# Retention and padded cross attention in quads of batches, and normalising in two parts at the end of three attentions

## The reference

```python
Q, K, V = x Wh, k Wh, v Wh                      # per head, 2 heads of 128 channels, k = v = ctx
scores = einsum('bshe,bthe->bhst', Q, K) / sqrt(hd)
masked = scores * Dn[None]                      # decay, per head
A = maximum(abs(masked.sum(axis=0)), 1.0)       # summed over ALL batches
O = einsum('hst,bthe->bshe', A, V).reshape(b, s, dim)
Y = (O - mean) / sqrt(var + 0.001) * gn_gamma + gn_beta
return (relu(x @ wg_w) * Y) @ wo_w
```

## Time and profile before

| | us |
|---|---|
| median of 3 runs (lowest, highest) | 2751.85 (2747.45, 2759.39) |
| profiled execution, whole | 2753.41 |
| its span, first to last instruction | 2751.5 |
| TensorE / VectorE / ScalarE / GpSimd busy, share of span | 81% / 68% / 48% / 13% |
| mean granted TensorE clock | 0.904 |

### The profile page before, as it was taken

One profiled execution on the slowest core, in us unless ns is written; L12 is line 12 of the kernel. 1 busy time (PEld: TensorE's weight loads), 2 busy tenths in 40 slices (PEclk: granted clock), 3 DMA queues, 4 the chain that ended last, 5 costly groups with the idle time before them and its releaser, 6 DMA issues. The chain is left out here.

```text
span 2751.5 us, 44570 instructions
## 1 busy us (share of the span) xinstructions
PE 2218.4 (81%) x18503; PEld 1701.3 (62%) x18503; DVE 1858.1 (68%) x3131; ACT 1326.3 (48%) x1718; POOL 348.9 (13%) x159
## 2 busy tenths in 40 slices
PE   7984268999999999999821896999999756787665
PEld 4663246777777777777721455999998433455443
DVE  5766756888877788887579442545454788587467
ACT  4652145666666666666433312333333346455237
POOL 0000112222322222232002320000000001100001
PEclk9997678999999999999965997999999877899878
DMA  3000022122122112221220642111100000000000
GB/s 140 2 1 13 9 74 53 49 60 57 47 59 78 55 51 59 51 55 48 62 96 0 188 118 99 42 26 46 34 31 0 9 1 1 22 2 1 16 1 31
DMA packets 159505, 122.81 MB, mean 45 GB/s; under 512 B 117728, under 2 KB 145120, under 8 KB 152800
## 3 DMA queue, kind: packets, MB, share of 16 engines
q1 hardware_dynamic: 156256, 116.00, 14.1%
q0 software_dynamic: 3072, 4.33, 0.9%
HBM read 102.62 MB, written 17.66 MB: 44 GB/s over the span
## 5 line engine op out<-in xcount | busy, mean ns | idle before, releaser
L1429 DVE SCALAR_TENSOR_TENSOR ctx_chan<-l1a_raw,l1a_cw,ctx_chan 128x1024 f32<-128x1024 f32 x192 | 230.8, 1278 | 19.5 <-ACT ctx_chan L1280 18.5
L1042 PE MATMUL banks<-x_chan,l1a_wp 128*128 128x512 f32 x512 | 230.4, 604 | 5.1 <-DMA l1a_wp<-in_l1a_wp_dram 5.1
L1006 POOL TENSOR_TENSOR l1a_sq<-ctx_chan 128x1024 f32<-128x1024 f32 x16 | 152.2, 9515 | 356.9 <-ACT ctx_chan L1284 356.9
L1042 PEld LDWEIGHTS banks<-x_chan,l1a_wp 128*128 128x128 f32 x512 | 98.0, 194 | 116.9 <-issue 110.7
L2531 PE MATMUL banks<-x_chan,l2a_wq 128*128 (+1 forms) x1024 | 123.7, 281 | 9.6 <-ACT l2a_ready L2396 4.9
L2531 PEld LDWEIGHTS banks<-x_chan,l2a_wq 128*128 128x128 f32 x1024 | 122.0, 198 | 11.2 <-issue 5.4
L1079 PE MATMUL banks<-l1a_wo,l1a_oT 128*128 128x256 f32 x512 | 121.8, 387 | 0.0
L1027 POOL TENSOR_TENSOR l1a_al<-l1a_aT,l1a_outer 128x1024 f32<-128x1024 f32 x32 | 74.8, 2360 | 330.2 <-DVE l1a_aT L1489 330.2
L2552 PE MATMUL banks<-l2a_wo,l2a_oT 128*128 128x256 f32 x512 | 113.2, 379 | 1.2 <-ACT l2a_oT L2420 1.2
L1050 PE MATMUL banks<-l1a_wz,x_chan 128*128 128x256 f32 x512 | 113.9, 381 | 0.0
L1050 PEld LDWEIGHTS banks<-l1a_wz,x_chan 128*128 128x128 f32 x512 | 97.9, 191 | 19.8 <-issue 7.2
(11 more groups left out here) (606 smaller groups left out, 5826.8 us busy)
## 6 DMA issues: line engine op xcount, KB each, us to landing
ctx_tok<-l1a_rows_mem SPq DMA_DIRECT2D x16, 1024.0 KB, 6.8
l1a_sq<-l1a_norm_mem SPq DMA_DIRECT2D x16, 1024.0 KB, 4.6
ctx_chan<-in_ctxT_dram SPq DMA_DIRECT2D x3, 2048.0 KB, 12.2
l1f_wgu<-in_l1f_wgu_dram SPq DMA_DIRECT2D x4, 1408.0 KB, 10.7
moe_sums<-l1x_zero SPq DMA_DIRECT2D x2, 2176.0 KB, 17.9
ctx_tok<-in_ctx_dram SPq DMA_DIRECT2D x2, 2048.0 KB, 11.6
l1a_wp<-in_l1a_wp_dram SPq DMA_DIRECT2D x8, 512.0 KB, 3.6
l1f_wgu<-moe_sums SPq DMA_DIRECT2D x8, 512.0 KB, 7.9
```

The source lines that it names most:

```text
L1006: P.tensor_tensor(sq[:, 0, :], conv[:, 0, :], conv[:, 0, :], ALU.mult).then_inc(s["k_squared"], 1)
L1042: mm = MM(ps[:, 2 * (u % 2) + q, :], wp[:, c, u * 128:(u + 1) * 128], g.xT[:, c, t0:t0 + 512], start=c == 0, stop=c == 1)
L1429: V.scalar_tensor_tensor(t, raw[:, u, :, j:j + S], cw[:, c, j:j + 1], t, ALU.mult, ALU.add).then_inc(s["conv_done" if step == 2 else "conv ...
```

## The change

In **`layer3_retention`** the weights of the projections get a semaphore of their own, and TensorE waits for that alone. Values are made between the projections, two projections and then one group of values; the scores of head 0 run in the middle of the projections. From there on the work goes in quads of four batches. TensorE alternates gate and application, ScalarE moves both to SBUF (the gate with its relu, in a new tile), GpSimd multiplies the gate by gamma and by beta (two tensor operations of 128x1024 for each quad), and VectorE needs two passes: (o - mean) * (gate * gamma), then that times the inverse deviation plus gate * beta. Statistics, gating, transposes, outputs and additions follow quad by quad, the final normalising in two parts, 0 to 11 and 12 to 15.

In **`layer0_cross`** the mask becomes a cap (one pass from the bytes), the scores take a minimum with it and the maximum in quads, and the subtraction of the maximum is folded into the exponentials as a bias. These run batch by batch with the sum as ScalarE's accumulated output. Transposes, copies, read outs and additions go by quads, and the division is ahead of the additions. The final normalising is in two parts.

In **`narrow_attention`** and **`layer2_attention`** the final normalising is in two parts, 0 to 11 (0 to 14) ahead of the last addition. In **`layer3_attention`** normalise(15) goes ahead of the first application, that covers 8 batches instead of 4 before the last addition, the table load goes behind wide_moved(15), and all turns go behind the last output.

```diff
# narrow_attention, ScalarE, VectorE
             wide_moved(B - 1)
+            A(g.scratch[:], g.ones[:, 0:1], ACT.Sqrt)
+            act_sqrt(act, g, s, 0, EARLY, 1)
             output_moved(B - 1)
-            act_norm(act, g, s["ln_mean"], s["ln_sqrt"])
-            act_turn_x(act, g, s["x_turned"], s["x_turned_out"])
+            act_turn_x(act, g, s["x_turned"], s["x_turned_out"], stop=DC * 2)
+            act_sqrt(act, g, s, EARLY, B, 2)
+            act_turn_x(act, g, s["x_turned"], s["x_turned_out"], first=DC * 2)
...
+            dve_moments(v, g, s, 0, EARLY)
             add(B - 2)
             normalise(B - 1)
+            dve_invert(v, g, s, 0, EARLY, 1)
+            dve_apply(v, g, s, 0, 2 * GROUP)
             add(B - 1)
-            v.wait_ge(s["added"], B)
-            dve_norm(v, g, s["ln_stats"], s["ln_mean"], s["ln_sqrt"], s["ln_out"], have_stats=True)
+            dve_moments(v, g, s, EARLY, B)
+            dve_apply(v, g, s, 2 * GROUP, EARLY)
+            dve_invert(v, g, s, EARLY, B, 2)
+            dve_apply(v, g, s, EARLY, B)
# layer0_cross, VectorE
+            V.tensor_scalar(cap[:], valid8[:], -2.0 * NEG, NEG, ALU.mult, ALU.add).then_inc(s["capped"], 1)
+            v.wait_ge(s["capped"], 1)
+            for q in range(QUADS):
+                masked(q)
+            V.tensor_reduce(anyv[:], cap[:], AX.X, ALU.max).then_inc(s["any_made"], 1)
...
+            for q in range(QUADS):
+                inverted(q)
+                if q:
+                    add(q - 1)
+            dve_moments(v, g, s, 0, EARLY)
+            dve_invert(v, g, s, 0, EARLY, 1)
+            dve_apply(v, g, s, 0, EARLY)
+            add(QUADS - 1)
# layer0_cross, ScalarE
+                for i in range(q * GROUP, (q + 1) * GROUP):
+                    ins = A(probs[:, i, :], sc[:, i, :], ACT.Exp, bias=rowmax[:, i:i + 1], scale=D ** -0.5, accum_out=rsum[:, i:i + 1])
...
+            exps(0)
+            exps(1)
+            probs_moved(0)
+            probs_moved(1)
+            exps(2)
+            exps(3)
+            A(g.scratch[:], g.ones[:, 0:1], ACT.Sqrt)
+            probs_moved(2)
+            probs_moved(3)
# layer2_attention, ScalarE, VectorE, TensorE
+                if last:
+                    A(g.scratch[:], g.ones[:, 0:1], ACT.Sqrt)
+                    act_sqrt(act, g, s, 0, EARLY, 1)
...
+            dve_moments(v, g, s, 0, EARLY)
+            dve_invert(v, g, s, 0, EARLY, 1)
+            dve_apply(v, g, s, 0, EARLY)
             add(B - 1)
...
+            pe.wait_ge(s["o_out"], 2 * B - 1)
+            pe_turn_x(pe, g, s["ln_out"], s["x_turned"], s["x_turned_out"], stop=DC)
             output(B - 1)
# layer3_attention, VectorE
             add(B - 2)
+            normalise(B - 1)
             invert(0, EARLY, 1)
-            layer_norm(0, GROUP)
-            normalise(B - 1)
-            layer_norm(GROUP, EARLY)
+            layer_norm(0, 2 * GROUP)
             add(B - 1)
             moments(EARLY, B)
+            layer_norm(2 * GROUP, EARLY)
             invert(EARLY, B, 2)
             layer_norm(EARLY, B)
# layer3_retention: GpSimd, then VectorE
+                pool.wait_ge(s["gate_out"], 2 * q + 2)
+                if q >= 2:
+                    pool.wait_ge(s["centred"], q - 1)
+                P.tensor_tensor(slopes[q % 2][:], quad, bc(gb[:, 0, :], 1, GROUP), ALU.mult).then_inc(s["sloped"], 1)
+                pool.wait_ge(s["sloped"], q + 1)
+                P.tensor_tensor(quad, quad, bc(gb[:, 1, :], 1, GROUP), ALU.mult).then_inc(s["offset"], 1)
...
+            def group_gated(q):
+                t0, t1 = q * GROUP, (q + 1) * GROUP
+                v.wait_ge(s["gn_sqrt"], q + 1)
+                V.reciprocal(rstd[:, t0:t1], rstd[:, t0:t1]).then_inc(s["gn_inverted"], 1)
+                v.wait_ge(s["sloped"], q + 1)
+                for t in range(t0, t1):
+                    ins = V.scalar_tensor_tensor(o[:, t, :], o[:, t, :], g.moments[:, t, 0:1], slopes[q % 2][:, t - t0, :], ALU.subtract, ALU.mult)
+                ins.then_inc(s["centred"], 1)
+                v.wait_ge(s["centred"], q + 1)
+                v.wait_ge(s["gn_inverted"], q + 1)
+                v.wait_ge(s["offset"], q + 1)
+                for t in range(t0, t1):
+                    ins = V.scalar_tensor_tensor(o[:, t, :], o[:, t, :], rstd[:, t:t + 1], gates[:, t, :], ALU.mult, ALU.add)
+                ins.then_inc(s["gated"], 1)
...
+            group_stats(0)
+            group_stats(1)
+            group_gated(0)
+            group_stats(2)
+            group_gated(1)
+            add(0)
+            group_stats(3)
+            group_gated(2)
+            add(1)
+            group_gated(3)
+            add(2)
+            moments(0, EARLY)
+            add(3)
+            normalise(0, EARLY, 1)
+            moments(EARLY, B)
+            normalise(EARLY, B, 2)
```

449 lines of the change are left out of this document (276 added, 173 removed).

## The result

| | before | after |
|---|---|---|
| median of 4 runs (lowest, highest), us | 2750.81 (2747.45, 2759.39) | 2718.85 (2718.33, 2729.73) |
| ratio, 95% interval | | 0.9888 [0.9859, 0.9916] |
| profiled execution, us | 2753.41 | 2729.73 |
| padded cross attention, start to start of the next sublayer | 47.1 | 37.1 |
| retention | 104.6 | 94.3 |

The change saves 32 us by the medians, 23 to 39 by the interval. The profiled execution of after is the slowest of its four and 23.7 us shorter than that of before; the stages of the table make up 23.5 of it. The other six sublayers differ by at most 2.4 us, in both directions.

A forecast was written before the change was run, and what follows sets the result against it. The prediction took the padded cross attention and retention to be chains, one engine working while others wait, and attention ends to normalise late. Terms 3.7 + 8.7 + 3.8 + 0.1 + 15.1 = 31.4 off 2753.4 gave 2722.0 us, range 2712 to 2736.

The forecast's parts named there:

- The fifth and largest term, the retention: Whole retention stage: work in quads removes the full passes, the gate's late half and waiting; 15.1 us saved, bounds 8 and 18.
- Padded cross attention: `layer0_cross`: VectorE's chain by quads, last turns done at 258.9 instead of 267.65; 8.7 us saved.
- the lower of the two bounds given: Padded cross attention, exponentials with accumulated output: nothing extra over 1.26 us for four; the upper bound, as much again each.
- First attention: End of the first attention: normalising in two parts, last turns done at 216.6 instead of 220.3; 3.7 us saved (2.5 to 4.5).
- Attention of layer 2: End of that attention: fifteen tiles normalised early, second square root waiting behind turns; 3.8 us saved (2.5 to 4.5).
- Attention of layer 3: End of that attention: VectorE was the bound and stays it; 0.1 us saved (0.8 lost to 0.8 saved).
- Retention to the end of the scores: Retention's first part: projection weights issued first, start at 2547.6 instead of 2551.47; scores end at 2577.5 against 2582.4.
- Retention after the scores: VectorE's chain of statistics, gating, additions and normalising by quads ends 54.2 us after the scores, before GpSimd's cost.
- GpSimd in it: Retention after the scores: GpSimd's eight new operations can hold up VectorE at the ports; priced at 2.0 us (0 to 8).
- Rival 2: Retention, GpSimd first at the ports: four operations each stop VectorE 2.3 us, 9.2 in all, giving 2729; chance 0.08.
- Relu: Retention's gate on ScalarE: relu shares the square root's table, costing nothing; otherwise six loads of 1.28 us.
- The other rivals: Low TensorE clock in retention (2734, chance 0.12); GpSimd starved (2766, 0.03); ends of layers 0 and 2 failing (2729.5, 0.08).

The follow-up runs named there:

- the version with GpSimd later: Changed kernel with GpSimd's retention operations for quads 2 and 3 waiting until quad 1's gating is done, the last until quad 2's; 2722.01 us, ratio 0.9876.
- the four named at `layer1_wkv`: Traces of the kernel before (twice), the three attention ends changed alone, and padded cross attention and retention changed alone; `layer1_wkv` took 106.5 to 106.8 us.

## Why the prediction was right, point by point

The forecast was 2722.0 in a range of 2712 to 2736; the median is 2718.85. It is right in direction and size, and the mechanism of four of the five parts is the forecast's. The fifth and largest term, the retention, was forecast at 15.1 us and measured at 10.2. That the total came within 3 us is partly luck: the padded cross attention and the ends saved more than forecast, an untouched sublayer gave some back, and the medians differ by 8 us more than the two profiled executions do.

- **Padded cross attention**, 8.7 forecast, 10.0 measured. The steps are the forecast's: VectorE's chain without a break, readouts and exponentials covered. From cap to last copy it had 34.4 us, and 33.2 were measured. A quad of masking is 1.53 us and not 1.64 (0.69 + 0.69 + 0.17), an addition in pairs 0.43 as taken, a statistic in pairs 0.33. The accumulated output costs little: four exponentials with their reads take 1.65 us from the first start to the last end, where L2704 took 1.26, nearer to the lower of the two bounds given, and hidden.
- **First attention**, 3.7 forecast, its end is 4.5 us shorter in the two profiled executions. The inversion came right behind normalise(15), the second square root was ready when asked for, and the last turn ended 9.4 after the division, 10.4 in one of the other kernels. That the stage shows only 1.7 in the first comparison is not the end's doing: the end began later.
- **Attention of layer 2**, 3.8 forecast, 4.8 measured (four traces with the old end, six with the new). The new wait was 1.76 us, not 2.3: the four turns ahead of the square root were copied in 2.4 us, and 2.8 was forecast. The step that failed is the sentence "The other seven sublayers are untouched": the cross attention behind it is longer by 2.4 us on the average and by 4.0 in the profiled execution, so the term was worth 2.4.
- **Attention of layer 3**, 0.1 forecast, 0.7 measured, and again not kept by the sublayer behind it.
- **Retention to the end of the scores**: forecast 32.1 us after its first instruction, measured 33.7. The first projections were at the low clock for longer than the 1.5 us allowed: by the records the first five took 0.84 to 1.22 us each, a later one takes 0.59.
- **Retention after the scores**: VectorE's chain was priced at 54.2 us without GpSimd, and is 52.7 in the version without it. The chain is right to 1.5 us, the pass of four at 1.64 to 1.67 too. (The text gives one operation in a row as 0.41 from L590's 16 in 6.84, which is 0.43; its 3.6 for eight goes by 0.43, and 0.41 is what was measured.)
- **GpSimd in it** is the mis-sized term: 2.0 forecast, 7.0 measured (59.7 less 52.7; 6.3 by the lengths of the stage). The bounds of 0 to 8 held it. With it the retention's shortfall of 5 us adds up: 1.6 us more ahead of the scores, 1.5 less in the chain, 5.0 more for GpSimd. The text placed one slip in gated(1), worth 2.3. What it missed is that slopes(2), and so offset(2) behind it, is released inside gated(0) and not after it, since the wait is on the first of the two passes: both operations run at VectorE's expense in quad 0, and both of the next in quad 1. The small operation of 128x4 was not thought of. Rival 2, with a chance of 0.08, had the right mechanism, four operations of GpSimd stopping VectorE, and its sign showed, operations of the gating over 0.5 us; of the 9.2 us that it gave them, and the 10.6 that VectorE was held in all, 7.0 reached the end of the chain.
- The two kinds of instruction of VectorE that were stopped are L3753, with two inputs of 128x256 in SBUF, and L3739, with one of 128x4. A statistic (L117) and an addition from a bank (L3761 of the version with GpSimd later) were not: 429 and 425 ns at most, with GpSimd beside them. The Trainium skill, "SBUF — State Buffer", section "Who interferes with whom", lists both kinds: two inputs in SBUF, and a tensor_scalar, which can enter a fast mode that takes both port pairs. The trace agrees for both: 2.57 us for 0.48, and 1.28 for 0.17. The prediction used only the first.
- **Relu**: taken at nothing, and there is no table load in the retention in any trace.
- The other rivals: GpSimd was not starved (2.35 to 2.58 us an operation), and TensorE stayed at the low clock for one quad of outputs only, 5.21 us for 3.72, beside VectorE's work.

Summed: 10.0 + 4.5 + 4.8 + 0.7 + 10.2 = 30.2 us of what was touched, against 31.4 forecast. In the two profiled executions 4.0 of it were given back in the layer-2 cross attention and 2.8 by the later start of the first attention's end, which comes within 0.4 of their difference of 23.7. The medians differ by 32; how much less the other executions gave back is not in any trace.

## What to carry to other kernels

Where GpSimd takes over elementwise work beside VectorE, look at which of VectorE's passes releases it: put its start behind the last pass with two SBUF inputs, so that it falls into reads of the banks and into waits. Read the maximum of a group of instructions and not its median, and look at small operations that are seven times too long. A microsecond saved at the end of a stage is only saved once the stage behind it has been measured with it.

## What was not expected of the hardware

- A VectorE operation on 128x4 float32 with one input, 0.17 us alone, took 1.28 us, until GpSimd's operation of 2.35 us ended. Its own size did not help it: it was held to the end of the other. The small operations of other kinds beside the same GpSimd operation were not held: L3736 took 0.15 to 0.18 us each, with GpSimd at work and without.
- GpSimd came in between VectorE operations that follow each other every 0.41 us, each time it was ready: two of its operations stretched a run of 1.67 us to 5.86 (the four took 0.49, 2.57, 2.57 and 0.47). In the kernel before, it had been the one to wait, 10.02 us.
- TensorE's clock: with twenty-four transposes that nothing reads (eight at the end of the attention, sixteen at the start of the sublayer) it was granted at 1.00 (2.4 GHz) over the first 10 us, where it had been 0.62 on the average, and the sublayer was no shorter, as later dips deepened.
- DMA landing: the 256 KB of wq took 2.7 us before and 3.5 after, issued in the same order at the start of the same sublayer. Over all traces it is 2.7 to 2.9 in the four named at `layer1_wkv` and 3.2 to 3.7 in the other nine.
